# Two layers' phases joined by early half products, and attention with split value products: one change to a one-core kernel of a state-space, MLP and attention stack

## The reference

```python
x = x + LN(mamba(LN(x)))        # projections, convolution, selective scan, W_out
x = x + LN(int_mlp(LN(x)))      # silu(x Wg * s) * (x Wu * s), then Wd * s; integer weights, 1376 wide
x = x + LN(attention(LN(x)))    # 32 query heads, 8 key/value heads of 128, low-rank K and V, partly rotary
x = x + LN(diff_mlp(LN(x)))     # 1792 wide; W = base + mean(|w - base|) * sign(w - base)
```

## Time and profile before

| | us |
|---|---|
| runs of the kernel before, median of 3 | 1802.15 (1801.33 to 1806.17) |
| the profiled execution, whole | 1799.71 |
| its span, first to last instruction | 1797.9 |
| PE busy in it | 1671.7 (93%) |
| DVE, ACT, POOL busy | 1101.3, 867.7, 812.4 |
| mean granted TensorE clock, share of full speed | 0.976 |

### The profile page before, as it was taken

How to read it: one execution, slowest core, us unless ns; L and a number is a source line. 1 busy time by engine, 2 the same in 40 slices (tenths; PEclk the granted TensorE clock), 3 DMA queues, 4 the chain that set the end, 5 groups by cost and what they waited for, 6 DMA issues and landing times. The chain is left out here.

```text
span 1797.9 us, 24221 instructions
## 1 busy us (share of the span) xinstructions
PE 1671.7 (93%) x8214; PEld 1374.2 (76%) x8214; DVE 1101.3 (61%) x1608; ACT 867.7 (48%) x1773; POOL 812.4 (45%) x414
## 2 busy tenths in 40 slices
PE   5995999999998799997998999999999999899998
PEld 4862788888886588786876888788787878788877
DVE  4337999999995433352915566665656667755422
ACT  2337777777763354233624454545444445543321
POOL 2212999999994373142612232222322225456333
PEclk9998999999999899998998999999999999899999
DMA  3203010101102393001200000100010010234100
GB/s 115 65 1 120 1 47 24 47 23 34 36 0 94 114 336 146 18 1 44 79 24 24 24 24 24 47 23 23 24 46 23 23 59 36 71 141 147 64 18 30
DMA packets 25188, 100.84 MB, mean 56 GB/s; under 512 B 3104, under 2 KB 3360, under 8 KB 22560
## 3 DMA queue, kind: packets, MB, share of 16 engines
q1 hardware_dynamic: 24976, 99.89, 15.6%
q10 hardware_dynamic: 144, 0.07, 0.0%
HBM read 97.72 MB, written 2.23 MB: 56 GB/s over the span
## 5 line engine op out<-in xcount | busy, mean ns | idle before, releaser
L1051 PE MATMUL psum<-scratch_s,res_const 128*128 128x256 f32 x1024 | 250.3, 382 | 4.3 <-DVE scratch_s L968 3.6
L1724 POOL TENSOR_TENSOR stretch_turned<-stretch_turned,res_const 128x1024 f32<-128x1024 f32 x32 | 79.4, 2481 | 359.5 <-ACT stretch_turned L1574 359.5
L1051 PEld LDWEIGHTS psum<-scratch_s,res_const 128*128 128x128 f32 x1024 | 191.7, 190 | 42.6 <-DVE scratch_s L968 17.9
L810 POOL TENSOR_TENSOR scratch_s<-scratch_s,scan_cm 128x1024 f32<-128x1024 f32 x64 | 151.0, 2359 | 32.1 <-DVE scratch_s L952 32.1
L1437 PE MATMUL psum<-opnd_xh,query_wqh 128*128 128x256 f32 x512 | 149.9, 293 | 8.9 <-POOL query_wql L1728 6.3
L952 DVE TENSOR_TENSOR_SCAN scratch_s<-psum,scratch_s 128x512 f32<-128x512 f32 x128 | 153.3, 1197 | 7.7 <-ACT psum L861 7.7
L798 POOL TENSOR_TENSOR scratch_s<-scan_bm,scratch_s 128x1024 f32<-128x1024 f32 x64 | 151.0, 2361 | 0.1
L1437 PE MATMUL psum<-opnd_xh,query_wql 128*128 128x256 f32 x512 | 144.8, 283 | 0.0
L1437 PE MATMUL psum<-opnd_xl,query_wqh 128*128 128x256 f32 x512 | 144.8, 283 | 0.0
L1045 PE MATMUL psum<-scan_diag,scratch_s 128*128 128x256 f32 x512 | 133.2, 384 | 6.6 <-ACT scratch_s L853 6.6
L1582 ACT ACTIVATE stretch_pa<-psum,stretch_nm 128x128 f32<-128x128 f32 x128 | 45.4, 366 | 178.2 <-DVE stretch_nm L1817 178.2
(11 more groups left out here) (298 smaller groups left out, 4296.3 us busy)
## 6 DMA issues: line engine op xcount, KB each, us to landing
mi_dw<-in_dw SPq DMA_DIRECT2D x24, 448.0 KB, 5.8
mi_dm<-in_dm SPq DMA_DIRECT2D x24, 448.0 KB, 6.4
query_raw<-in_w_q SPq DMA_DIRECT2D x8, 1024.0 KB, 4.7
query_raw<-in_w_o SPq DMA_DIRECT2D x8, 1024.0 KB, 4.8
scan_cm<-bc_rows SPq DMA_DIRECT2D x12, 512.0 KB, 4.3
gu_raw<-in_w_gu SPq DMA_DIRECT2D x11, 512.0 KB, 7.7
mlpa_raw<-in_w_mlp SPq DMA_DIRECT2D x7, 768.0 KB, 4.3
mlpa_base<-in_b_mlp SPq DMA_DIRECT2D x7, 768.0 KB, 5.9
```

Of the source, the lines that this page charges most:

```text
L810: nc.gpsimd.tensor_tensor(shared[r][h], shared[r][h], weights(4 * h, 4), ALU.mult).then_inc(weighted_pool, 1)
L1051: mm = nc.tensor.matmul(ps_y[r], ident, part[:, n * SEQ:(n + 1) * SEQ], start=False, stop=stop and (n + 1) * SEQ == part.shape[1])
```

## The change

Four things are done. (1) `finish_phase` gets `next_split` and `next_products`: fa splits the weights of mi's steps 0 and 1 (ACT at its steps 2 and 3, DVE at 3 and 4), and fb those of kv's steps 0 to 2. PE makes the products of the following phase for the first 512 tokens: one before the transposes of tile 6, one before those of tile 7, the rest at the end (four in fa, three in fb, 12 matmuls of 128x512 each). The two phases' banks in PSUM are moved so that the products can stay, and the following phase makes only the second half of these steps (`first`). (2) In mi SP requests the weights of step f+2 in step f, ahead of the differences, and ACT's order becomes prepare(f+1), Silu(f), differences(f). kv's first three requests wait for nothing. (3) In attention the three f32 value products become nine fp32r ones of split values (`vh` on ACT, `vl` on POOL) and split probabilities (`ph` on ACT, `pl` on DVE); the transposes of the probabilities (`flips`) go to the banks of the scores and stand between the first 18 and the last 6 output matmuls; DVE's two accumulations are taken apart; the copy of values goes. (4) POOL makes the low parts of the query and output weights in two halves, and PE waits for each half where it needs it; the output lows also wait for the maxima of unit 4g+1. Fewer buffers are used: `direct` shares `q`, and half of `oh` and `ol` share `ph` and `pl`.

```diff
@@ finish_phase @@
+    next_in, next_hi, next_lo = sem("next_weights_in"), sem("next_weights_hi"), sem("next_weights_lo")
...
-    ps_y = [M.ps[:, i, :] for i in range(2)]
-    ps_t = [M.ps[:, 2 + i, :] for i in range(2)]
+    ps_y = [M.ps[:, 2 * i + 1, :] for i in range(2)]
+    ps_t = [M.ps[:, 2 * i + 5, :] for i in range(2)]
...
+            def next_product(i):
+                bank, split, hi, lo = next_products[i]
+                pe.wait_ge(next_hi, split + 1)
+                pe.wait_ge(next_lo, split + 1)
+                at_least(pe, x_lo, TT // 2)
+                for k in range(KM):
+                    for j, (w, x) in enumerate(((hi, M.xh), (hi, M.xl), (lo, M.xh))):
+                        nc.tensor.matmul(M.ps[:, bank, :], w(k), x[:, k, 0:HALF], start=(k == 0 and j == 0),
+                                         stop=(k == KM - 1 and j == 2))
...
+                if next_products and TT <= t < TT + 2:
+                    next_product(t - TT)
                 if not store and t >= lag:
                     transposes(t - lag, (t - lag) % 2)
             for t in range(TT + (0 if store else lag)):
                 step(t, t % 2)
+            for i in range(2, len(next_products)):
+                next_product(i)
...
+                if 0 <= t - 2 < len(next_split):
+                    raw, hi, _ = next_split[t - 2]
+                    act.wait_ge(next_in, 16 * len(next_split))
+                    nc.scalar.activation(hi, raw, ACT.Copy).then_inc(next_hi, 1)
...
+                if 0 <= t - 3 < len(next_split):
+                    raw, hi, lo = next_split[t - 3]
+                    dve.wait_ge(next_hi, t - 2)
+                    nc.vector.tensor_tensor(lo, raw, f32(hi), ALU.subtract).then_inc(next_lo, 1)
@@ widen_phase, SP @@
+                elif exists(f + 2, F):
+                    at_least(sp, w_lo, f + 1 - done)
+                    sp.dma_start(raw[s][:, :], raw_dram[:, cols(f + 2, RC)]).then_inc(raw_in[s], 16)
                 if diff is not None and exists(f, N_SUMS):
                     at_least(sp, d_abs, f * 3 - 3)
@@ widen_phase, PE @@
+                first = 1 if isinstance(f, int) and f < done else 0
...
-                            for h in range(2):
+                            for h in range(first, 2):
@@ widen_phase, ACT @@
-                if exists(f + 1, F):
+                if exists(f + 1, F) and not (isinstance(f, int) and f + 1 < done):
                     prepare(f + 1, 1 - s)
-                if diff is not None and exists(f, N_SUMS):
+                if diff is not None and exists(f, N_SUMS) and done == 0:
                     differences(f, s)
...
                     nc.scalar.activation(m[:, :], ps[s][0], ACT.Silu, scale=sc).then_inc(first_done, 1)
+                    if diff is not None and done:
+                        if exists(f, N_SUMS):
+                            differences(f, s)
+                        if isinstance(f, int) and f >= 7:
+                            next_highs(f)
@@ key_value_phase @@
-                sp.wait_ge(w_lo, it - RING + 1)
+                at_least(sp, w_lo, it - 2 * RING + 1)
...
-                        for h in range(2):
+                        for h in range(1 if f < RING else 0, 2):
@@ attention_mlp_phase, PE @@
+                    if b == 0 and h == 2:
+                        at_least(pe, wq_lo, 2 * g)
...
+            def output(g, b, t, first=0, end=HPG):
...
+                if first == 0:
+                    at_least(pe, added, v * 2 - 1 + t)
+                for h in range(first, end):
+                    if b == 0 and t == 0 and h == 2:
+                        pe.wait_ge(wo_lo, 2 * g + 2)
...
+            def attend(g, b):
+                v = g * BATCH + b
+                pe.wait_ge(v_hi, v + 1)
+                pe.wait_ge(v_lo, v + 1)
+                at_least(pe, o_lo, v * 2)
+                for i, (bank, keys) in enumerate(((X[2], 0), (X[0], 0), (X[0], 1))):
+                    pe.wait_ge(p_hi, v * 3 + i + 1)
+                    if i == 1:
+                        at_least(pe, added, v * 2 - 1)
+                    nc.tensor.matmul(bank, vh[:, keys, :], ph[:, i, :], start=(i < 2), stop=False)
+                    nc.tensor.matmul(bank, vl[:, keys, :], ph[:, i, :], start=False, stop=False)
+                pe.wait_ge(p_lo, v * 3 + 1)
+                nc.tensor.matmul(X[2], vh[:, 0, :], pl[:, 0, :], start=False, stop=True).then_inc(summed, 1)
+                pe.wait_ge(p_lo, v * 3 + 3)
+                nc.tensor.matmul(X[0], vh[:, 0, :], pl[:, 1, :], start=False, stop=False)
+                nc.tensor.matmul(X[0], vh[:, 1, :], pl[:, 2, :], start=False, stop=True).then_inc(summed, 1)
...
+                early = HPG if ending(g, b, BATCH - 1) else HPG // 2
...
+                    output(*behind, 0)
+                    output(*behind, 1, 0, early)
+                flips(g, b)
+                if any_behind and early < HPG:
+                    output(*behind, 1, early)
                 attend(g, b)
@@ attention_mlp_phase, POOL @@
                 pool.wait_ge(wo_hi, g + 1)
-                nc.gpsimd.tensor_tensor(flat(wol), raw[:, :], f32(flat(woh)), ALU.subtract).then_inc(wo_lo, 1)
+                pool.wait_ge(neg_max, g * BATCH + 2)
+                for h in (slice(0, 2), slice(2, HPG)):
+                    nc.gpsimd.tensor_tensor(wol[:, h, :], raw[:, :].rearrange("p (h c) -> p h c", h=HPG)[:, h, :],
+                                            f32(woh[:, h, :]), ALU.subtract).then_inc(wo_lo, 1)
...
+                if more(g, b):
+                    values_low(*after(g, b))
@@ attention_mlp_phase, DVE @@
+                if behind:
+                    accumulate(v - 1, (b - 1) % BATCH, 0)
+                for i in range(3):
+                    dve.wait_ge(p_hi, v * 3 + i + 1)
+                    nc.vector.tensor_tensor(pl[:, i, :], turned_p[i], f32(ph[:, i, :]), ALU.subtract).then_inc(p_lo, 1)
...
                 if more(g, b):
                     rotate(*after(g, b))
+                if behind:
+                    accumulate(v - 1, (b - 1) % BATCH, 1)
```

More of the change, by code:

```diff
@@ L644, in step @@
             def step(f, s):
-                if kind == "int" and exists(f + 1, F):
+                if kind == "int" and exists(f + 1, F) and not (isinstance(f, int) and f + 1 < done):
                     int_lows(f + 1, 1 - s)
@@ L669, in _ @@
                 whole(0, 0)
-            if kind == "int":
+            if kind == "int" and done == 0:
                 int_lows(0, 0)
@@ L1145, in key_value_phase @@
     vwh, vwl = place("vwh", [P, KM, VC], F32R), place("vwl", [P, KM, VC], F32R)
-    wh = [place(f"wh{i}", [P, KM * P], F32R) for i in range(RING)]
-    wl = [place(f"wl{i}", [P, KM * P], F32R) for i in range(RING)]
+    split = len(items) - RING
     turned = [spare(f"turned{i}", [P, TOK]) for i in range(2)]
```

205 lines of the change are left out of this document (110 added, 95 removed).

## The result

The changed kernel takes 1791.4 us (median of 6 runs, 1789.91 to 1793.36) against 1801.8 for the kernel before in the same session: a ratio of 0.9937, 95% interval 0.9922 to 0.9952. It is faster by 0.6%, or 10 us. I had forecast 33 us and a range of 1757 to 1784: the sign is right, the size is a third, and the range missed it.

What follows compares the result with a forecast made beforehand. TensorE, busy 1671.7 of 1797.9 us, was taken as the bound. Terms of +1.5 (fa, mi), -10.3 (fb, kv) and -24 (attention) sum to -32.8: 1766.9 from the profiled 1799.71, forecast 1769 as median, range 1757 to 1784.

Steps and rivals of the forecast that it cites:

- the signs that I had named for being wrong: Wrong if mi ends more than 3 us earlier, relative to fa's start, or plain attention units stay above 17.7 us.
- Part 2: End of fb and start of kv: three moved products and a warm start give -10.3 us (bounds -7 and -11).
- Part 1: End of fa and start of mi: 11 us of matmuls taken out come back as a stall, +1.5 us.
- The stall: Ahead of mi's third step: TensorE idles 11 us until VectorE's low half of the weights, then starts cold.
- The splits added to fa's steps: In fa: two ScalarE copies and two VectorE subtractions, costed at nothing; without cover 2 x 1.2 us.
- Part 3: Attention: split value products, new order and halved lows give -24 us (bounds -8 and -30).
- the plain unit: An attention unit when nothing is late: bound by TensorE, 17.34 us instead of 17.86.
- a new wait of 1.1 us: Attention unit b=1: TensorE waits for the output low's halves, now behind the maxima, 1.1 us (bounds 0 and 1.5).
- the edges: Both ends of the attention phase: the f32 values at a cold clock get shorter, -1 us.
- B: Rival, attention: bound by its chain, every unit loses 0.5 us, part 3 is -8, time 1785; chance 0.12.
- C: Rival, attention: the split form of the value products gains nothing, 17 us are missing, time 1786; chance 0.05.
- D: Rival, attention: copies, lows and rotation in series between transposes and scores; slower, 1811 at 1.3 us a unit; chance 0.04.

Runs made afterwards that it cites:

- e9: Changed kernel with the maxima wait only ahead of the output lows' second half, and three f32 value products replacing nine split ones: 1786.7 us.
- e13: Changed kernel, fa's ScalarE weight copies moved to idle time, both VectorE lows to fa's end, early products using high weights for low: 1792.7 us.
- e1: Changed kernel with the wait for the maxima taken from the output lows, both halves made at once: 1776.3 us.
- e3: Changed kernel with the maxima wait only ahead of the output lows' second half, plus four unread GpSimd subtractions behind it: 1798.0 us.

## Why the prediction was wrong, step by step

None of the signs that I had named for being wrong came: mi did not end earlier, and the plain units are under 17.7 us. What failed lay where I had named no sign.

**Part 2** was right in its mechanism: -10.35 for -10.3. From kv's first matmul to attention it is 102.86 us instead of 112.53, and nothing took the place of the matmuls removed. That it agrees to 0.05 us is luck. fb was not free of cost either: from the end of its first step (17.65 us behind its start, 18.61 before) to the transposes of the last tile it is 57.55 us instead of 56.60, 0.95 us more, with the split of 3.44 us in it. As in fa the added splits are the likely cause; no run shows it for fb alone. The first step was 0.96 us shorter and hid it; in e9, where it is 18.69, the stretch is 183.88 us and not 182.85.

**Part 1** came out at +5.6 for +1.5. The stall was right in place, cause and length: 22.5 us from mi's first matmul to its third step, where I had 22.3. The failed step is "The splits added to fa's steps ... I cost at nothing". I looked for the cover of a product two steps later on TensorE, not for what stood behind each split on its own engine: on ScalarE the copy stood ahead of the next hidden tile's high copy, on DVE the subtraction ran into POOL's low. By e13 that is 2.8 of the 3 us; the other 0.3 is fa's first step. The last 0.8 is the step behind the stall, which took 14.1 us (645.41 to 659.52, at a granted clock of 0.78) and not 13.3.

**Part 3** was right for the plain unit (17.25 for 17.34; e9 gives the price of the split alone), for b=2, and for TensorE's waits in b=1 (0.98 for 1.1). The failed step is "That is a new wait of 1.1 us (bounds 0 and 1.5)". It counts who waits for the halves, but not what the halves lie over. I had their place at S+3.75 to S+8.4 and the end of the scalings at S+9.45 on the same page and did not put them side by side. The bound of 1.5 was therefore wrong in kind. In seven groups it was 19.84 - 18.4 = 1.4 us too little each, some 10 us; the last group's 24.40 is 6 more. The rest of the miss is the end: from the last queries on, the last two units take 45.5 us instead of 41.8, 3.7 more, where I had -1 for the edges. In the last one TensorE waits 5.33 us for the scalings (4.56 before) and 2.86 us for the output operand's low part (0.54 before). Of these 3.7 us, 1.6 come back at once, and they are the -1.6 of the table's last line: TensorE then waits only 0.23 us for the next normed tile, where it waited 1.83 before.

Behind this is a misread row. I put b=1's 0.81 us in the kernel before down to an accumulation behind POOL's low, because the bracket named it. The trace of the kernel before had the real place, in that unit:

```profile
1047.80 1.31 DVE L1817 TENSOR_SCALAR stretch_nm<-stretch_mx 128x8 f32<-128x8 f32 x1
```

The 128x8 product that makes the negative maxima stands until POOL's low ends (1044.47 + 4.62 = 1049.09), all the exps follow, and an accumulation is merely the last in that chain. e1 shows the same, 1.79 us.

The Trainium skill, "SBUF — State Buffer", section "Who interferes with whom", says that VectorE's tensor_scalar in its 2-port mode and a GpSimd instruction exclude each other for a whole instruction, and that the one issued second waits. The rows agree on who waits and how long: 0.17 became 1.79 us, and one 128x128 scaling 3.53 us beside a 3.50 us subtraction. In which mode an instruction ran no row shows. I had quoted this section for two-input subtractions alone; it lists tensor_scalar too.

**The rivals.** None named this. B came nearest to part 3 (-8 for -3.15), but in a wrong place (every unit by 0.5 us); what happened is one unit in four by 2.6. C is out by e9. D asked only for work in series on one engine.

## What to carry to other kernels

When work moves on GpSimd, draw its interval over VectorE's whole list of that stretch. In these traces the scalings, and the subtractions of two SBUF tiles, waited for its end, and the dearest was the tiny one that a whole chain hangs on. A wait that keeps it off one of them has to be checked against the next; here a wait between two halves kept it off both, and was worth 20 us where a wait ahead of both cost them. And a split that is "covered" has three engines to be covered on: ask on each what stands behind it in program order. And a term that agrees to a tenth may be two errors that cancel: cut the stretch once more, at a mark that repeats from run to run.

## What was not expected of the hardware

- VectorE instructions differ under the same GpSimd subtraction. In e1 the second addition of the masks (PSUM and SBUF in, PSUM out) began at 1109.44, 0.4 us behind POOL's start, and kept its 0.69 us, as did the reductions behind it, and in the changed kernel the reciprocal of 128x8 kept its 0.20 us at 1117.31; the 128x8 product beside them went from 0.17 to 1.79.
- GpSimd loses next to nothing in return. Its 3.50 us subtraction over the waiting scalings was 3.51 in the kernel before, the sine 2.35 to 2.43 with scalings beside it and 2.41 without, and e3's subtractions of 256 columns took 0.77 us each (median), another of that size (the value's low) 0.73.
- Short VectorE instructions got in one at a time. In the last group's b=1 four scalings took 7.29 us, from 1476.53 to past the end of the sine at 1483.53: their lengths (0.27 to 3.53 us) fit one passing at each boundary between GpSimd's instructions, though GpSimd had its next one ready.

What stays open: the length of the first step or unit of a phase, which falls on different values although nothing in it or ahead of it was changed (fa starts anywhere from 553.66 to 557.66 us, its first step takes 13.95 to 15.0 us, fb's 17.6 to 18.9, attention's first queries 16.3 to 18.7), and when the clock falls behind a wait, as in five of e3's units and not in two. No run here explains them. Differences of 1 to 2 us between single profiles are not read as effects unless they are counted behind such a first step.
